# Gate and up products of a gated feed-forward with seven block products instead of eight

## The reference

```python
x = x + tanh(g_xattn[0]) * xattn(layernorm(x), ctx, mask)   # softmax(q @ ctx.T / sqrt(512)) @ ctx
x = x + tanh(g_ffn[0]) * ffn(layernorm(x), w_gate, w_up, w_down)

def ffn(x, w_gate, w_up, w_down):         # 512 -> 2048 -> 512
    h = silu(x @ w_gate) * (x @ w_up)
    h_sparse = sparsify_2to4(h)           # of each 4 neighbours keep the 2 with the largest |h|
    return h_sparse @ w_down
```

## Time and profile before

| | |
|---|---|
| median of three runs | 1212.21 us |
| span of the profiled execution | 1210.4 us |
| TensorE matmul busy | 1189.7 us, 98% |
| VectorE busy | 755.0 us, 62% |
| ScalarE busy | 428.7 us, 35% |
| GpSimd busy | 103.4 us, 9% |
| DMA, mean | 66 GB/s |

### The profile page before, as it was taken

How to read it: one execution, slowest core, us unless ns; L and a number is a source line. 1 busy time by engine, 2 the same in 40 slices (tenths; PEclk the granted TensorE clock), 3 DMA queues, 4 the chain that set the end, 5 groups by cost and what they waited for, 6 DMA issues and landing times.

```text
span 1210.4 us, 15963 instructions
## 1 busy us (share of the span) xinstructions
PE 1189.7 (98%) x5344; PEld 954.2 (79%) x5344; DVE 755.0 (62%) x1289; ACT 428.7 (35%) x788; POOL 103.4 (9%) x281
## 2 busy tenths in 40 slices
PE   7998989999999999999999999999999999999998
PEld 6776768888888888888888888888888888888887
...
GB/s 238 264 240 189 95 105 35 35 35 35 35 35 70 1 131 8 35 35 35 35 35 69 0 139 31 4 35 35 35 35 69 35 1 69 69 69 69 69 35 70
DMA packets 40245, 80.48 MB, mean 66 GB/s; under 512 B 2720, under 2 KB 19104, under 8 KB 35616
## 3 DMA queue, kind: packets, MB, share of 16 engines
...
...
## 4 chain that ended last, share of the span: by engine, by line
PE 88%; DVE 1%; ACT 0%; issue 0%; ACTq 0%; DVEq 0%
PE ps_y L62 10%; PE ps_y L63 10%; PE ps_y L64 10%; PE ps_up L62 10%; PE ps_gate L62 10%; PE ps_up L63 10%; PE ps_up L64 10%; PE ps_gate L63 10%; PE ps_gate L64 10%; DVE beats L735 0%; ACT h_hi L722 0%; DVE part L769 0%; DVE part L770 0%; DVE rows L742 0%; DVE hidden L781 0%; DVE wins L773 0%
## 5 line engine op out<-in xcount | busy, mean ns | idle before, releaser
L753 DVE TENSOR_TENSOR hidden<-ps_up,silu 128x512 f32<-128x512 f32 x128 | 88.4, 691 | 412.2 <-PE ps_up L64 411.0
L702 ACT ACTIVATE hidden_abs<-hidden 128x512 f32<-128x512 f32 x128 | 81.0, 633 | 375.0 <-DVE hidden L753 375.0
L62 PE MATMUL ps_gate<-x_hi,gu_hi 128*128 128x512 f32 x496 | 196.9, 397 | 3.3 <-ACT silu L700 3.3
L63 PE MATMUL ps_gate<-x_lo,gu_hi 128*128 128x512 f32 x496 | 197.0, 397 | 0.0
L64 PE MATMUL ps_gate<-x_hi,gu_lo 128*128 128x512 f32 x496 | 196.9, 397 | 0.0
L62 PE MATMUL ps_y<-dn_hi,h_hi 128*128 128x512 f32 x496 | 196.3, 396 | 0.0
L63 PE MATMUL ps_y<-dn_lo,h_hi 128*128 128x512 f32 x496 | 196.2, 396 | 0.0
L64 PE MATMUL ps_y<-dn_hi,h_lo 128*128 128x512 f32 x496 | 196.2, 396 | 0.0
L62 PE MATMUL ps_up<-x_hi,gu_hi 128*128 128x512 f32 x496 | 196.2, 395 | 0.0
L63 PE MATMUL ps_up<-x_lo,gu_hi 128*128 128x512 f32 x496 | 196.1, 395 | 0.0
L64 PE MATMUL ps_up<-x_hi,gu_lo 128*128 128x512 f32 x496 | 195.9, 395 | 0.0
...
## 6 DMA issues: line engine op xcount, KB each, us to landing
x_raw<-xnT_scratch SPq DMA_DIRECT2D x32, 1024.0 KB, 4.8
x_in<-in_x SPq DMA_DIRECT2D x32, 256.0 KB, 3.0
ctx_in<-in_ctx SPq DMA_DIRECT2D x32, 256.0 KB, 3.1
xnT_scratch<-x1nT SPq DMA_DIRECT2D x32, 256.0 KB, 2.8
out_rows<-rows SPq DMA_DIRECT2D x7, 1024.0 KB, 5.0
gu_raw<-in_L_ffn_w_gate SPq DMA_DIRECT2D x4, 1024.0 KB, 5.1
gu_raw<-in_L_ffn_w_up SPq DMA_DIRECT2D x4, 1024.0 KB, 7.3
gu_raw<-in_L_ffn_w_down SPq DMA_DIRECT2D x4, 1024.0 KB, 6.6
```

Source lines behind the costliest of these rows:

```text
L62: nc.tensor.matmul(bank, a_hi, b_hi, start=start, stop=False)
L63: nc.tensor.matmul(bank, a_hi, b_lo, start=False, stop=False)
L702: nc.scalar.activation(hidden_abs[:, j], hidden[:, j], ACT.Abs).then_inc(abs_done, 1)
L753: nc.vector.tensor_tensor(hidden[:, j], ps_up[j % 2][:], silu[:, j % 2], ALU.mult).then_inc(hidden_done, 1)
```

## The change

The kernel is written anew around the gate and up products. 1024 rows by the 512 inputs are taken as two by two blocks (two halves of 512 rows, two halves of the 512 inputs), and so are the weights, with gate and up each cut in two halves of inputs; the 2 x 2 x 2 block product is made with seven products of sums of blocks instead of eight (a scheme of Winograd's form). For that

- the weights become seven tiles of block sums for each unit `u` (half of the j of a quarter: `e` = 0, 1 stands for one j each), and the rows seven sums for each pair `p` of half blocks. The first eight units are built while the pair p = 0 runs (`spread`, `w_sum`, `w_high`, `w_low`), stored to `w_scratch` and loaded again for later pairs (`load_w`); the rows of the next pair are made at five points of a step (`x_point`), stored to `xm_scratch` and loaded at the pair's end (`load_xm`);
- there are 4 pairs x 4 quarters = 16 steps of two units each. A unit is 7 products x 2 (e) x 2 chunks x 3 matmuls. Behind each unit from the third on stands the down product of one half (512 rows, 48 matmuls) of the step before;
- products add up in PSUM in six banks (`ps_a`, `ps_c`, `ps_d`, for two e); partial sums are copied out by ScalarE (`copy_a0`, `copy_a1`, `copy_d0`) before the bank goes on, and VectorE adds them (`add_c11`, `add_c22`, `add_c12`, then `gated0`, `gated1`). Two banks are left for y instead of four;
- only 8 of 32 residual rows stay in SBUF, the others go to DRAM and come back a pair at a time; down's split factors are stored in pair 0 and loaded later, in pair 0 their upper parts are made by ScalarE (`dn_high`) and their lower ones by GpSimd;
- the attention's slots are all written out. In them the first unit's weights are built (raw pieces of 512 KB in one buffer `w_raw`, each asked for when the one before is spread) and the first pair's rows; the lower parts of both are made by VectorE in the slot after ScalarE made the upper ones. ScalarE begins the feed-forward when the last stores of the attention have landed.

The core of the diff; the dots leave out the rest:

```diff
+W_FROM = (0, 1, 0, 4, 2, 1, 3)
+X_FROM = (0, 2, 3, 0, 1, 3, 2)
+X_TO = (0, 1, 5, 3, 4, 2, 6)
+X_AT = {m: i for i, m in enumerate(X_TO)}
...
+ORDER = (1, 0)
+SPREAD0 = {2: 0, 3: 1, 4: 2, 5: 3}
+W0_AT = {6: 0, 7: 1, 9: 2, 10: 3, 11: 4, 12: 5, 13: 6}
+S0_AT = {6: (0, 1), 8: (2,), 9: (3,)}
+SPREAD1 = {15: 0, 16: 1, 17: 2, 18: 3}
+X0_AT = {17 + i: (0, i) for i in range(7)} | {26 + i: (1, i) for i in range(7)}
...
+        def spread(act, u, blk):
+            act.wait_ge(w_raw_loaded, 16 * (4 * u + blk + 1))
+            wait(act, w_lo_done, 7 * u)
+            g = u % 2
+            nc.scalar.activation(w_blk[:, blk], w_raw[:].rearrange("p c (m j) -> p j c m", j=GROUP)[:, 2 * g:2 * g + 2],
+                                 ACT.Copy).then_inc(spread_done, 1)
+        def w_high(act, u, k):
+            if k in (0, 1, 6):
+                act.wait_ge(spread_done, 4 * u + (1, 2, 0, 0, 0, 0, 4)[k])
+            else:
+                act.wait_ge(sums_done, 4 * u + (0, 0, 3, 1, 2, 4)[k])
+            if u > 0:
+                act.wait_ge(made[k], 2 * u)
+                act.wait_ge(w_stored[k], 16 * u)
+            nc.scalar.activation(w_ring[:, k, :, 0], w_blk[:, W_FROM[k]], ACT.Copy).then_inc(w_hi_done, 1)
...
+        def w_low(engine, instructions, u, k):
+            engine.wait_ge(w_hi_done, 7 * u + k + 1)
+            instructions.tensor_tensor(w_ring[:, k, :, 1], w_blk[:, W_FROM[k]], w_ring[:, k, :, 0].bitcast(F32),
+                                       ALU.subtract).then_inc(w_lo_done, 1)
...
+        def w_sum(dve, u, i):
+            if i == 0:
+                dve.wait_ge(spread_done, 4 * u + 4)
+                nc.vector.tensor_tensor(w_blk[:, 4], w_blk[:, 2], w_blk[:, 3], ALU.add).then_inc(sums_done, 1)
...
+        def x_point(s, point):
+            n = 5 * (s % QS) + point
+            if s // QS == PAIRS - 1 or n >= 14:
+                return None
+            return s // QS + 1, n // 7, n % 7
...
+            def load_w(u, k):
+                sp.wait_ge(made[k], 2 * u)
+                if u == BUILT:
+                    sp.wait_ge(w_stored[k], 16 * BUILT)
+                sp.dma_start(w_ring[:, k].rearrange("p e h c m -> p (e h c m)").bitcast(F32), w_dram[u % BUILT, k]
+                             ).then_inc(w_loaded[k], 16)
...
+            def load_dn(s):
+                wait(sp, y_done, 2 * TILES * s)
+                if s < QS:
+                    if s == 0:
+                        sp.wait_ge(down_copied, 16)
+                    else:
+                        sp.wait_ge(dn_stored, 16 * s)
+                    sp.dma_start(dn[:, 1].rearrange("p j n -> p (j n)").bitcast(F32), raw_dram[s]).then_inc(dn_raw_loaded, 16)
...
+                    sp.dma_start(xnT_dram[h // 2, :, :, (h % 2) * HALF:(h % 2) * HALF + HALF], x1nT[:, h % 2]
+                                 ).then_inc(xnT_stored[h % 2], 16)
+                if n in SPREAD0 and n - 2 < 3:
+                    load_w_piece(sp, 0, n - 1)
+                if n - 1 in W0_AT:
+                    store_w(0, W0_AT[n - 1])
+                if n in SPREAD1:
+                    load_w_piece(sp, 1, SPREAD1[n])
+                if n == 16:
+                    load_x_blk(sp, 0, 0)
+                if n == 24:
+                    load_x_blk(sp, 0, 1)
+            load_x_blk(sp, 1, 0)
+            load_w_piece(sp, 2, 0)
...
+            for s in range(STEPS):
+                p = s // QS
+                u = 2 * s + 1
+                if u < BUILT:
+                    if s > 0:
+                        for blk in range(1, 4):
+                            load_w_piece(sp, u, blk)
+                        if u + 1 < BUILT:
+                            load_w_piece(sp, u + 1, 0)
+                    for k in range(PROD):
+                        store_w(u, k)
+                else:
+                    for k in range(PROD):
+                        load_w(u, k)
...
-            slots(act, slot)
+                if n in SPREAD0:
+                    spread(act, 0, SPREAD0[n])
+                if n in W0_AT:
+                    w_high(act, 0, W0_AT[n])
+                if n in SPREAD1:
+                    spread(act, 1, SPREAD1[n])
+                if n in X0_AT:
+                    x_high(act, 0, *X0_AT[n])
...
+            for s in range(STEPS):
+                u = 2 * s
+                building = u + 1 < BUILT
+                if s > 0:
+                    absolute(s - 1, 1, 0)
+                copy_a0(u, 0)
+                if s > 0:
+                    absolute(s - 1, 1, 1)
+                copy_a0(u, 1)
+                if s > 0:
+                    h_high(s - 1, 0, 0)
+                    h_high(s - 1, 0, 1)
+                    absolute(s - 1, 1, 2)
+                    absolute(s - 1, 1, 3)
+                    h_high(s - 1, 0, 2)
+                    h_high(s - 1, 0, 3)
+                if 0 < s <= QS:
+                    for j in range(GROUP):
+                        dn_high(s - 1, j)
+                silu0(u, 0)
+                silu0(u, 1)
+                if building and s > 0:
+                    spread(act, u + 1, 0)
+                copy_a1(u, 0)
+                if building and s > 0:
+                    spread(act, u + 1, 1)
+                copy_a1(u, 1)
+                copy_d0(u, 0)
+                if building and s > 0:
+                    spread(act, u + 1, 2)
+                copy_d0(u, 1)
+                if building and s > 0:
+                    spread(act, u + 1, 3)
+                if building:
+                    w_high(act, u + 1, 0)
+                    w_high(act, u + 1, 1)
+                if s > 0:
+                    for j in range(GROUP):
+                        h_high(s - 1, 1, j)
+                silu1(u, 0)
+                silu1(u, 1)
+                if building:
+                    for k in range(2, PROD):
+                        w_high(act, u + 1, k)
+                x_high_at(s, 0)
+                u = 2 * s + 1
+                building = u + 1 < BUILT
+                copy_a0(u, 0)
+                copy_a0(u, 1)
+                absolute(s, 0, 0)
+                absolute(s, 0, 1)
+                silu0(u, 0)
...
+            for s in range(STEPS):
+                u = 2 * s
+                building = u + 1 < BUILT
+                if s > 0:
+                    keep(s - 1, 0)
+                add_c11(u, 0)
+                add_c11(u, 1)
+                if s > 0:
+                    for j in range(GROUP):
+                        h_low(s - 1, 0, j)
+                    compare(s - 1, 1, FIRST + REST)
+                add_c22(u, 0)
+                add_c22(u, 1)
+                if s > 0:
+                    count_wins(s - 1, 1)
+                add_c12(u, 0)
+                add_c12(u, 1)
+                if s > 0:
+                    keep(s - 1, 1)
+                    for j in range(GROUP):
+                        h_low(s - 1, 1, j)
+                gated0(u, 0)
+                gated1(u, 0)
+                gated0(u, 1)
+                gated1(u, 1)
+                if building and s > 0:
+                    w_sum(dve, u + 1, 0)
+                    w_sum(dve, u + 1, 1)
+                if s > 0:
+                    add_y(s - 1, 0, 0)
+                if building:
+                    w_low(dve, nc.vector, u + 1, 0)
+                    w_sum(dve, u + 1, 2)
+                    w_low(dve, nc.vector, u + 1, 1)
+                    w_sum(dve, u + 1, 3)
+                if s > 0:
+                    add_y(s - 1, 0, 1)
+                if building:
+                    w_low(dve, nc.vector, u + 1, 2)
+                    w_low(dve, nc.vector, u + 1, 3)
+                if s > 0:
+                    add_y(s - 1, 0, 2)
+                if building:
+                    w_low(dve, nc.vector, u + 1, 4)
+                    w_low(dve, nc.vector, u + 1, 5)
+                    w_low(dve, nc.vector, u + 1, 6)
+                if s > 0:
+                    add_y(s - 1, 0, 3)
...
+            bank = (ps_a, ps_c, ps_a, ps_d, ps_a, ps_d, ps_a)
+            def product(u, k, e):
+                p = u // (2 * QS)
...
+                    if u == 0:
+                        pe.wait_ge(neg_scores_done, B)
+                if k == 2:
+                    pe.wait_ge(a0_copied[e], u + 1)
+                if k == 3:
+                    wait(pe, c12_done[e], u)
+                    if u == 0:
+                        pe.wait_ge((pT_copied, nT_copied)[e], B)
+                if k == 4:
+                    pe.wait_ge(a1_copied[e], u + 1)
+                if k == 5:
+                    pe.wait_ge(d0_copied[e], u + 1)
+                if k == 6:
+                    pe.wait_ge(c22_done[e], u + 1)
+                to = bank[k][e][:]
+                begins = k in (0, 1, 3)
+                for c in range(2):
+                    nc.tensor.matmul(to, w_ring[:, k, e, 0, c], xm[:, k, 0, c], start=begins and c == 0, stop=False,
+                                     skip_group_check=not begins)
```

(30 more changed lines are left out.)

1204 lines of the change are left out of this document (636 added, 568 removed).

## The result

The changed kernel takes 1309.95 us (median of 4 runs, 1309.12 to 1311.47), the kernel before 1212.58 in the same hour: 1.0807 times as long, 95% interval 1.0792 to 1.0823. The prediction said 1259, between 1185 and 1292: slower was right, the size was not. The profiled execution has a span of 1308.4 us, 51.3 more than the sum's 1257.1.

The account below looks back on a forecast made before the run. Time was set by when the attention frees TensorE and by every matmul or stall after: start 158.6 + matmuls 985.5 + building 78.8 + steady 18.7 + end 12 + last store 3.5 = 1257.1 us profiled, median 1259, range 1185 to 1292.

Parts of the forecast that it names:

- slots 15 to 18: Attention: rounds of piece loads beside other loads, and two slots with a split, give some 9 us (4 if pieces are timely).
- The count, 4224: Feed-forward: 384 fewer matmuls, 4224 in all, a gain of 89.6 us, all on the path if nothing stalls.
- Their price, 0.2333: Feed-forward: one matmul of 512 columns costs 0.2333 us, so 4224 take 985.5 us.
- Start at 155: End of attention: the first product begins at 155 us (158.6 less half clock), right from 150 to 162.
- Building units, 78.8: Steps 0 to 4, where units also make the next one's factors: queue waits add 78.8 us of stalls.
- VectorE 95% busy in steps 1 and 2: Building steps 1 and 2: VectorE's load is 57 us a step and a little, so it is 95% busy.
- Steady stall 1.7, eleven times: Steps 5 to 15: down's tile 2 waits 1.7 us for the first y addition in even units, 18.7 in all.
- The end, 12: Last two halves of down, with no unit beside them: waits for VectorE cost 12 us, between 8 and 16.
- Transfers hidden at nothing: From unit 8 on: loads of factors and rows, and stores with steps of slack, cost nothing.
- Piece, 3.6 to landing: Raw weight pieces of 512 KB: estimated to land 3.6 us after being asked, 4.8 with spread and issue.
- Rival A: ScalarE's queue in slots 2 to 5, 15 to 18 and units 1 to 6: doesn't block, 1161 us; chance 0.26.
- Rival B: Upper bound's costs too (down tile behind stores, late rows, instruction fetching): 78.8 becomes 105, 10 at pairs, 1295; chance 0.12.

Follow-up runs that it names:

- e1: The kernel before with every register loop written out, nothing else changed: 1210.81 us, ratio 0.9992.
- e10: The changed kernel with attention pieces asked one slot ahead of their spreads, spreads two slots apart, and the last down tile loaded early: 1296.26 us.
- e3: The changed kernel without making, storing and loading the rows' block sums for pairs 1 to 3 (wrong output, one execution): 1261.74 us.
- e8: The changed kernel with ScalarE's spreads behind the copies TensorE waits for in steps 0 to 4, and VectorE's odd-unit gating and win count moved: 1286.06 us.
- e11: The changed kernel with the orders of e7 and e8, ScalarE asking for pieces itself on its own queue, and x sums moved: 1244.2 us.
- e7: The changed kernel with VectorE adding the first y tile before the four gating multiplications in even units: 1291.08 us.

## Why the prediction was right or wrong

The step that failed is the walk of the in-order queues, in the building units (78.8 of stalls) and in slots 15 to 18 of the attention (9). It let an instruction wait for operations and for a piece that lands 3.6 us after it is asked, and left out that the request itself waits its turn on SyncE, that a part of x waits for a store, and most of the half clock behind waits. The runs showed 124.0 in place of 78.8, and a first product at 172.83 in place of 155. A second error hid part of this: the price of a matmul was too high. With 0.2267 the same sum gives 1229, so the terms that were too small missed by some 80 and not by 51. One by one:

- **The count, 4224, and that every matmul saved is on the path:** right. **Their price, 0.2333:** wrong, 0.2267, a gain of 28 us over all of them that the sum lacked. I had taken the pace of the earlier trace rows as the engine's own. It is a matter of where two tensors lie. That the changed kernel has the fast distance everywhere is luck, as nobody had looked for it, and the first step of the kernel before ran at 2.72 already; one more pair of lines there would have shown two paces and put the question.
- **Start at 155:** wrong, 172.8. The gain of 5 for unrolled slots is not to be seen in e1, whose span is 1.1 shorter than the kernel's before. The term "slots 15 to 18, some 9" was the largest miss: ScalarE's four spreads there waited 22.5 us. I walked them as rounds of 4.8, while each piece is asked in the same slot as its spread, among that slot's loads and stores, and ScalarE waited up to 8.9 for one. e10 takes most of these waits away and starts at 155.56.
- **Building units, 78.8:** the mechanism was right (copies behind spreads that wait for pieces, `x_high` in front of copy_a0 in unit 2: I had 7.0, the row 7.51). The size was not, 124.0. Three waits were missing: a part of x waits for the store of the one before, since x_out is single (23.1 us of ScalarE's waits there; e3 prices the parts of x as a whole); SP asks for pieces only after stores that wait in order (the rows of e8, and e11); the raw down tile lands 7.6 after its issue and stood in front of copies (the row at 253.06, 22.4 us of ScalarE's waits; alone it was not tried). I had put the last in the upper bound only. All three belong to queues that I had walked for their operations and not for their waits. The fourth term is half clock: 42.3 us where the walk had some 10. I had charged it behind a handful of waits, and put "2.6 of half clock after each longer wait" into the upper bound; the view of waits has 27 there. (Unit 4's parts add to its 13.0 only without VectorE's 3.1.)
- **VectorE 95% busy in steps 1 and 2:** wrong, 52.3 of 90.6 us in TensorE's step 1 (58%) and 59.8 of 94.5 in step 2 (63%), the stretches from 230.05 to 320.66 and from there to 415.14, as the steps had become longer than its load.
- **Steady stall 1.7, eleven times:** right, 1.55 at that place in nine of the eleven steps, and e7 removes it by the order that the prediction had named.
- **The end, 12:** 11.0 above the bare pace, right in size but by luck, as the profile has another cause (and the waits named in the prediction, 4.7, 3.1 and 0.3 with a half clock of 2.6, add to 10.7). The load of the last tile can only be asked once down(14) is done, and no unit hides it; I had not walked SP there. e10 shows that the cause I had given stood just behind.
- **Transfers hidden at nothing:** right from unit 10 on but for 2.8 us of late down tiles and 4.9 at unit 17.
- **Piece, 3.6 to landing:** medians of 4.1 (gate) and 3.6 (up) in the trace after, near enough alone, but behind others in the queue up to 9.8 to landing. The fit of the Trainium skill ("DMA: Bandwidth & Descriptors", section "Anatomy of one DMA"), made there for transfers that GpSimd issues, works out to an estimate of 3.2 for 512 KB. No piece here, asked by SyncE, landed in less than 3.5.
- **Rival A (queues don't block):** excluded by 124 us of stalls where it had 18. Its point of decision, when copy_a1 of the second tile ends, was the right one to look at: L586 ends 60.4 us of TensorE's idle time.

**Rival B (upper costs, 1295):** nearest to the result and still 15 short. Its chance of 0.12 was too low for one reason: the walk had a lower and an upper bound for loads and pieces, none for the waits that in-order queues pass on to each other, and these only add.
